# A convolution's input laid out in 64 lanes in place of 16, read by TensorE in shifted windows

## What is computed

```
y = x + conv1d(x, w, 9 taps, padding 4, 4 groups of 32 channels) + (cond @ c_weight.T)[:, :, None] + bias
h = gelu(gelu(cond @ W0 + b0) @ W1 + b1);  att = softmax(h @ W2 + b2)           # 8 weights per sample
z = y + (sum_k att[k] * weight[k]) @ y + (att @ bias_k)[:, :, None]             # 128 x 128 per sample
```

## Time and profile before

| | |
|---|---|
| median of 3 runs | 734.4 us (734.14 to 735.44) |
| span of the profiled execution (its own time) | 734.3 us |
| PE busy | 724.5 us (99%) |
| PE weight loads | 706.8 us (96%) |
| ACT busy | 545.7 us (74%) |
| POOL busy | 483.9 us (66%) |
| DVE busy | 413.2 us (56%) |
| DMA | 177.56 MB, 242 GB/s |

### The profile page before, as it was taken

The page is one execution under the profiler, slowest core; times in us unless marked ns, Lnnn a source line. Parts: engine busy times, 40 slices in busy tenths (PEclk is TensorE's granted clock), DMA queues, the critical chain, the costliest instruction groups (busy, mean ns, idle before and its releaser), DMA issues.

```text
span 734.3 us, 29222 instructions
## 1 busy us (share of the span) xinstructions
PE 724.5 (99%) x12417; PEld 706.8 (96%) x12417; DVE 413.2 (56%) x411; ACT 545.7 (74%) x458; POOL 483.9 (66%) x592
## 2 busy tenths in 40 slices
PE   8999999999999999999999999999999999999996
PEld 6898898899999999999999999999999999999996
DVE  3877557456466465465465465465465465465443
ACT  4878777787777777777777777777777777777743
POOL 2699999857876755755755756756756656656640
PEclk8999999999999999999999999999999999999999
DMA  6356766777877787777678776777777777777546
GB/s 222 132 172 215 247 226 229 241 270 259 280 248 249 254 277 256 243 274 269 234 255 292 250 259 241 246 258 245 244 254 253 245 253 252 240 251 259 189 139 250
DMA packets 66551, 177.56 MB, mean 242 GB/s; under 512 B 7437, under 2 KB 50008, under 8 KB 50264
## 3 DMA queue, kind: packets, MB, share of 16 engines
q1 hardware_dynamic: 66002, 176.93, 70.4%
q10 hardware_dynamic: 518, 0.17, 0.1%
HBM read 101.57 MB, written 75.50 MB: 241 GB/s over the span
## 4 chain that ended last, share of the span: by engine, by line
PE 81%; POOL 12%; DMA 4%; issue 1%; SPq 1%; DVE 0%; ACT 0%; POOLq 0%; DVEq 0%; ACTq 0%
PE ps L429 59%; PE ps L460 22%; POOL mix_prod L744 5%; POOL mix_prod L739 4%; DMA mix_dram<-mix_parts 2%; POOL mix_sum_f L747 1%; DMA x_in<-in_x_dram 1%; POOL mix_parts L754 1%; POOL mix_f L751 1%; POOL mix_parts L757 1%; DMA mix_rep<-mix_dram 0%; SPq L290 0%; POOL par L734 0%; POOL par L731 0%; ACT x_hi L512 0%
## 5 line engine op out<-in xcount | busy, mean ns | idle before, releaser
L429 PE MATMUL ps<-x_hi,cw_hi 32*128 32x512 f32 x3072 | 421.9, 392 | 1.5 <-ACT x_hi L512 1.5
L429 PE MATMUL ps<-x_hi,cw_lo 32*128 32x512 f32 x3072 | 417.5, 388 | 0.0
L612 DVE TENSOR_TENSOR y_lo<-ps,y_hi 128x512 fp32r<-128x512 f32 x256 | 159.1, 684 | 296.6 <-ACT y_hi L521 296.6
L429 PE MATMUL ps<-x_lo,cw_hi 32*128 32x512 f32 x3072 | 280.5, 388 | 0.0
L508 ACT ACTIVATE x_ph<-x_in 128x2176 f32<-128x2176 f32 x63 | 266.6, 4233 | 2.1 <-DMA x_in<-in_x_dram 2.0
L429 PEld LDWEIGHTS ps<-x_lo,cw_hi 32*128 32x128 f32 x3072 | 248.0, 183 | 3.6 <-issue 0.8
L429 PEld LDWEIGHTS ps<-x_hi,cw_hi 32*128 32x128 f32 x3072 | 222.5, 184 | 5.3 <-issue 1.8
L429 PEld LDWEIGHTS ps<-x_hi,cw_lo 32*128 32x128 f32 x3072 | 222.2, 184 | 2.9 <-issue 0.2
L460 PE MATMUL ps<-y_hi,mix_rep 32*128 32x512 f32 x2048 | 217.7, 385 | 0.7 <-DMA mix_rep<-mix_dram 0.7
L534 ACT ACTIVATE z_out<-ps,par 128x1024 f32<-128x1024 f32 x124 | 143.8, 1218 | 77.5 <-PE ps L460 77.5
L521 ACT ACTIVATE y_hi<-ps 128x512 fp32r<-128x512 f32 x256 | 132.8, 603 | 92.0 <-PE ps L429 91.9
(11 more groups left out here) (79 smaller groups left out, 89.3 us busy)
## 6 DMA issues: line engine op xcount, KB each, us to landing
x_in<-in_x_dram SPq DMA_DIRECT2D x64, 1024.0 KB, 7.0
out_dram<-z_out SPq DMA_DIRECT2D x63, 1024.0 KB, 4.8
mix_rep<-mix_dram SPq DMA_DIRECT2D x256, 128.0 KB, 2.7
mix_dram<-mix_parts SPq DMA_DIRECT2D x64, 128.0 KB, 5.1
out_dram<-x_in SPq DMA_DIRECT2D x2, 512.0 KB, 3.5
z_out<-in_L_cond_weight_dram SPq DMA_DIRECT2D x1, 512.0 KB, 4.0
cw_nat<-in_L_cond_weight_dram SPq DMA_DIRECT2D x1, 144.0 KB, 2.3
w_sb<-in_L_cond_W_dram ACTq DMA_DIRECT2D x2, 64.0 KB, 5.2
```

What stands on the lines that cost most here:

```text
L429: mm = pe.matmul(y_at(s)[:, g, :], w[rows, m, :], x_at(xx[buf(s)], rows, m), start=i == 0, stop=i == CONV - 1)
L612: nc.vector.tensor_tensor(y_lo[s[1]][:, g, :], y_at(s)[:, g, :], y_hi[s[1]][:, g, :].bitcast(F32), ALU.subtract).then_inc(y_lo_made, 1)
```

## The change

One constant. A phase is stored as 64 lanes of 8 blocks, plus 2 blocks of overlap: 10 x 64 = 640 elements in place of 544. A block is 64 x 4 = 256 bytes and a phase 2560 bytes, where it was 64 and 2176. The reads of x_in by by_lane, and the writes of z_out by out_lanes, have strides of 32 elements in place of 128. Each engine's instructions and their order are the same; only the shapes of x_ph, x_hi and x_lo grow, from 128x2176 to 128x2560.

```diff
@@ -61,7 +61,7 @@
     M = K + PH - 1
     ROUNDS = NS // U
     PC = NK + 1
-    LANES = 16
+    LANES = 64
     H = N // LANES
     CONV, MIX = 3 * M, 3 * G
     STEPS = CONV + MIX
```

## The result

| | before | after |
|---|---|---|
| median of 5 runs | 734.65 us (734.14 to 735.73) | 728.89 us (727.84 to 730.09) |
| ratio | | 0.9917, 95% interval 0.9905 to 0.9929 |
| span of the profiled execution | 734.3 us | 726.9 us |

The change makes the kernel 5.8 us faster, 0.8%, and the interval leaves out no change. The page of the changed kernel: PE's share and chain, and the groups whose tiles grew.

What follows compares the result with a forecast made beforehand. TensorE was taken as the bound, busy 99%, with late GpSimd and SyncE's circle limiting before 144.25 us. 734.3 - 8.3 + 2.2 = 728.2, plus 0.1 for the median: 728.3 us; range 724.2 to 732.5.

Steps and rivals of the forecast that it cites:

- TensorE, -8.3 us from 52 slots: From 144 us to the end, all rounds take 226.9 ns, each slot 0.16 us less: -8.3 us over 52 slots.
- ScalarE: x_ph grows by 0.75 to 4.98 us at the same 1.95 ns an element; idle time takes it and nothing waits.
- DVE and GpSimd, +4.2 us for matrix 5: Seven longer VectorE pairs, 0.6 us each, hold GpSimd in the beginning; the matrix of sample 5 is stored at 89.4 us.
- Its copy at 101.2 us, PE stopped for 3 us: Sample 5's matrix copy begins 7.8 us after its store, lands at 101.2 us; TensorE stalls there about 3 us.
- Last stop ends at 146.5 us: TensorE's stall at sample 9 ends at 146.5 us, the middle of 144.8 to 148.5: +2.2 us to 144.25.
- "DVE itself is busy 56%; that hides it": VectorE's longer cast and subtraction, +0.6 us a pair, are hidden because that engine is busy only 56%.
- The sum: The profiled span of 734.3 us less 8.3 plus 2.2 gives 728.2; the median stands 0.1 above, so 728.3 us.
- A: Rival: full gain without early loss, sample 9 still arriving near 144.3 us; 726.1 us, or 724; chance 0.17.
- B: Rival: half of the 4.3 ns between round kinds belongs to something else, gain 4.2 us; 732.4 us; chance 0.1.
- C: Rival: round length hangs on the mix of shifted reads, no gain, longer copies only; 736.7 to 738.6 us; chance 0.1.
- D: Rival: ScalarE becomes the bound if x_ph exceeds 6.7 us; 790 us at 3 ns a word; chance 0.03.

Runs made afterwards that it cites:

- e7: The changed kernel with only the weights (mix_rep, cw_hi, cw_lo) moved by 64 bytes, x and y left in place: 744.79 us in one timed run.
- e2: The kernel with 32 lanes, in place of 16 before the change: blocks of 128 bytes, phases of 2304; 730.33 us, ratio to before 0.9939.
- e8: The changed kernel with x_lo of samples 2 to 7 made for phase 0 alone, which leaves out work: 724.83 us, ratio to before 0.9857.
- e11: The changed kernel with one GpSimd operation less for each matrix, the identity being added as the matrices leave PSUM: 726.62 us, ratio to before 0.9899.
- e12: The changed kernel itself, measured again side by side with the version that has one GpSimd operation less per matrix: 728.01 us, ratio to before 0.9921.
- e1: The changed kernel, 64 lanes, with 128 bytes of padding between the phases of x_hi and x_lo: 736.24 us, ratio to before 1.0027.
- e3: The changed kernel with y_hi and y_lo moved by 64 bytes against x_hi and x_lo: 733.61 us, ratio to before 0.9988.
- e5: The changed kernel with every tile in SBUF moved by 64 bytes: 725.95 us in one timed run.
- e6: The changed kernel with every tile in SBUF moved by 128 bytes: 726.86 us in one timed run.
- e4: The changed kernel with SyncE's order in a slot made load_mix, load, store_mix, store, the store going last: 729.54 us, ratio to before 0.9932.
- e10: The kernel before (16 lanes) with phases and weights padded so each tap's window and own weights begin alike modulo 256: 734.29 us, ratio 0.9996.
- e9: The changed kernel with the 1 MB load and store issued from ScalarE's queue, SyncE's carrying the matrices alone: 731.18 us, ratio to before 0.9952.

## Why the prediction was right

**728.3 us was forecast, 728.89 measured**, and the sign and the range hold. So does the mechanism in its two main terms, faster rounds by the place of the reads and a late GpSimd in the beginning; several sizes are right in part by luck. Point by point:

- *TensorE, -8.3 us from 52 slots.* The slot was put at 10.89 and is 10.880; 52 x 0.167 = 8.7 us. The 226.9 ns came from rounds in the same trace, and that was the right row. The reason given was wrong in part: "the place" was taken for the place of the windows relative to y's. It is the place relative to the weights (e7), which in this kernel happens to be the same. With the weights 64 bytes elsewhere the changed kernel takes 744.79 us, more than the kernel before has with its weights in place (734.64).
- *ScalarE.* x_ph put at 4.98 us, 5.06 measured; the stride of 128 bytes costs what that of 512 does (5060 / 2560 = 1.98 ns, before 1.95, 1.93 in e2 at 256 bytes). ScalarE isn't the bound, with 0.28 us a slot to spare at its narrowest place.
- *DVE and GpSimd, +4.2 us for matrix 5.* 89.4 forecast, 89.13 measured, of two terms that were both off. GpSimd was to start 0.2 us later and started 0.3 sooner (its first copy from the table at 22.96, before at 23.28), and from there to the end of matrix 5 it took 4.7 us more. The seven pairs of DVE grew by 6.0 us together, 0.86 each in place of 0.6, because beside GpSimd they are longer than the free ones that the forecast went by (x_lo 3.5 us, 2.8 free), and not all of it held GpSimd up. e8 and e11, in which matrix 5 goes with what DVE or GpSimd has to do (ready at 75.1 and 86.2 us), confirm the link.
- *Its copy at 101.2 us, PE stopped for 3 us.* PE went on at 99.94, 1.4 us later than it would have been there. The step that failed: the 7.8 us from store to copy were taken as fixed, and they were 94.25 - 89.13 = 5.1 us. They fit the load of the queue: before, the 2 MB went out just ahead of the matrix; now they left 4 us earlier, while SP waited.
- *Last stop ends at 146.5 us.* 144.85 was measured, at the low end of 144.8 to 148.5: +0.6 in place of +2.2 us. This term was mis-sized: 11.54 us for each matrix, the upper bound of the sum, was put down to SP's circle, and from matrix 5 to 9 it ran at (131.56 - 89.13) / 4 = 10.6 us. The profile of e12 has its last wait for a matrix at 142.88 us.
- *"DVE itself is busy 56%; that hides it".* This failed in slots 1 to 3, where DVE has no idle time from 26.1 to 53.9 us. PE waits for x_hi of sample 2 at 35.1 us, and at 46.6 us for y_lo of sample 2, which begins as x_lo of sample 3 ends; with the long rounds behind these waits it is 1.05 us more than before. A share over the span says nothing of the first three slots. DVE, then PE, in order of time:

```profile
42.57 3.25 DVE L601 TENSOR_TENSOR x_lo<-x_ph,x_hi 128x2560 fp32r<-128x2560 f32 x1
45.74 2.47 DVE L612 TENSOR_TENSOR y_lo<-ps,y_hi 128x512 fp32r<-128x512 f32 x4
```

```profile
46.56 0.47 PE L429 MATMUL ps<-x_hi,cw_hi 32*128 32x512 f32 x1 [0.28 <-DVE y_lo L612]
```

- *The sum.* In spans the forecast was 728.2 and 726.9 was measured, 1.3 us too high. The forecast took span and time as equal, since the profiled execution of before had a span of 734.3 near the median time of its runs; but in the runs since, a time is 2.0 to 2.2 us above its span (728.89 and 726.9), so the old profile was probably of a longer execution than the median. That the medians agree to 0.6 us is to this extent luck.
- *Rivals.* A (no early loss) is out as a whole: there are 3.14 us of stops against 1.28, and its 726.1 us was not measured. But half of its condition came true, the faster circle, with sample 9 at 144.85 where A had 144.3; in spans the gain of 7.4 us lies between the forecast's 6.1 and A's 8.3. B is out: the whole difference went (all rounds 226.7 ns), so 256 bytes are enough. C is what e1 built: the longer copies without the gain, 736.2 us, forecast 736.7, and the sign was right. Its reason (a round hangs on the mix of shifted reads) is out as the only one, by e2, e3 and e7. D is out by the 5.06 us of x_ph. The Trainium skill (TensorE: Matmul & The Clock Gate, Back-to-back issue gap) has no term for an address; here the same four matmuls take 226.7 or 233.3 ns by the address alone. What the Trainium skill says of the shared port (SBUF — State Buffer, Who interferes with whom) is that a VectorE instruction with two SBUF inputs contends with a GpSimd one that reads SBUF. These traces agree: GpSimd's matrices were 4.3 us later when DVE's pairs had grown by 6.0 us. The 3.00 us of the earlier trace rows stand beside a subtraction that took 3.40 us there, from 59.30 us on, and not the free 2.42.

## What to carry to other kernels

Where TensorE is the bound with a fresh weight load for each matmul, compare the starting addresses of its moving reads and of its weights modulo 256: all alike was the fastest of what was tried here. It was had by the sizes of block and phase, without touching the weights, and one gap of 128 bytes between the phases took it away (e1). Look for such a term by comparing rounds of the same kernel that differ in nothing else, and then move one side alone, since two tiles that move together prove nothing. An engine's share over the span hides its first slots, where a late start leaves it no idle time; sum what the change adds there separately.

## What the runs showed of the hardware

- Four row-tiled matmuls of 32 rows and 512 columns, each with its own weight load, take 226.7 ns together if moving reads and weights begin at the same place modulo 256 bytes (at three such places, e5, e6 and the change), 233.3 when the weights stand 64 bytes off (e7), 228.9 when y stands 64 bytes off the other way (e3), 233.3 at 128 bytes once settled (e2, rounds 24 to 27). At a granted clock of 0.50 the rounds took 427 ns, in the kernel before, with its reads at two places 128 bytes apart (10.6 to 13 us), as in e4 with its reads at one (83.5 to 86.4 us).
- Alike to the matmul's own weights isn't enough (e10, a slot of 11.04 us); that it is another tap's weight load that counts is likely and not shown.
- A read of one word every 128, 256 or 512 bytes costs ScalarE nearly the same, 1.98, 1.93 and 1.95 ns an element with the fixed part (the change, e2, before).
- 128 KB copies landed after 6.0 us (median) when the big transfers were issued from another queue (e9), and after 2.7 us when they went ahead of them in the same one (the change).
- How long GpSimd is held goes by DVE's operations beside it: the same two L744 operations took 2.11 us free and 5.11 us beside a pair, and DVE's x_lo beside GpSimd 3.5 us, 2.8 free (the change).
